# Adaptive-norm transformer block: reduce steps over all units, dense steps in two halves, a fixed table of stages, values and causal rows by DMA

## What is computed

```python
h = _layernorm(x) * (1 + ca) + sa
x = x + ga * attention(h)      # 16 heads of 16, causal, q/k/v/o each w plus a LoRA of rank 16
h = _layernorm(x) * (1 + cb) + sb
x = x + gb * ffn(h)            # relu(base + lora_e) @ Wo.T, the two best of 4 experts, weighted
```

## Time and profile before

| | |
|---|---|
| median of 3 runs | 2076.18 us (2071.84 to 2076.54) |
| profiled execution | 2072.05 us, span 2070.3 us |
| PE, DVE, ACT, POOL busy | 1851.8, 1232.0, 940.3, 507.7 us |
| granted PE clock, mean | 0.96 |

### The profile page before, as it was taken

How to read it: one execution, slowest core, us unless ns; L and a number is a source line. 1 busy time by engine, 2 the same in 40 slices (tenths; PEclk the granted TensorE clock), 3 DMA queues, 4 the chain that set the end, 5 groups by cost and what they waited for, 6 DMA issues and landing times.

```text
span 2070.3 us, 31214 instructions
## 1 busy us (share of the span) xinstructions
PE 1851.8 (89%) x10868; PEld 951.2 (46%) x10868; DVE 1232.0 (60%) x2729; ACT 940.3 (45%) x1701; POOL 507.7 (25%) x803
## 2 busy tenths in 40 slices
PE   5788987999889998899979999799988999799958
PEld 4433443445444454354634545344544545344526
DVE  5666768555774557755585556755578545764241
ACT  1255555444454445544454454544445444454320
POOL 5112211332113321223113221132211332122213
PEclk8879998999999999999999999999999999999979
DMA  4412221121211121111211122012121112110100
GB/s 134 126 42 73 63 57 32 54 68 54 62 45 54 43 86 44 37 62 57 67 32 52 57 65 60 23 56 67 59 58 51 54 65 67 32 32 11 36 0 21
DMA packets 103667, 111.88 MB, mean 54 GB/s; under 512 B 20214, under 2 KB 97618, under 8 KB 103516
## 3 DMA queue, kind: packets, MB, share of 16 engines
q1 hardware_dynamic: 103500, 109.87, 17.8%
q10 hardware_dynamic: 16, 0.02, 0.0%
HBM read 75.72 MB, written 33.58 MB: 53 GB/s over the span
## 4 chain that ended last, share of the span: by engine, by line
PE 65%; DVE 24%; ACT 5%; issue 3%; DMA 1%; SPq 1%; POOL 0%; POOLq 0%; DVEq 0%; ACTq 0%
PE dense L924 10%; PE ov L844 10%; PE st L829 8%; PE mxs L813 7%; DVE negm L1235 6%; PE dense L935 5%; DVE negm_left L1235 5%; PE dense L859 5%; PE dense L901 5%; PE dense L909 4%; PE dense L794 3%; ACT probs L983 3%; PE mxs L817 2%; DVE stats L1087 2%; DVE second L1303 1%
## 5 line engine op out<-in xcount | busy, mean ns | idle before, releaser
L983 ACT ACTIVATE probs<-st 128x512 f32<-128x512 f32 (+1 forms) x1216 | 665.4, 576 | 543.2 <-PE st L829 537.1
L1235 DVE TENSOR_REDUCE negm<-mxs 128x1 f32<-128x384 f32 (+4 forms) x736 | 431.5, 614 | 176.9 <-PE mxs L817 175.1
L829 PE MATMUL st<-q_st,k_st 98*128 98x512 bf16 (+3 forms) x1536 | 455.2, 337 | 29.0 <-ACT probs L983 14.9
L813 PE MATMUL mxs<-k_st,q_st 96*128 96x512 bf16 (+3 forms) x1280 | 400.8, 328 | 57.3 <-DVE negm L1235 33.7
L1235 DVE TENSOR_REDUCE negm_left<-mxs 128x1 f32<-128x512 f32 x512 | 334.7, 683 | 101.6 <-PE mxs L813 98.6
L844 PE MATMUL ov<-probs,v_g 128*32 128x512 f32 (+3 forms) x3072 | 337.9, 511 | 4.7 <-POOL probs L703 4.6
L813 PEld LDWEIGHTS mxs<-k_st,q_st 96*128 96x128 bf16 x1280 | 126.6, 99 | 334.3 <-DVE negm L1235 154.9
L924 PE MATMUL dense<-c_t,wi_t 128*128 128x512 f32 x512 | 245.3, 601 | 0.7 <-ACT ratio_b L1035 0.7
L700 POOL TENSOR_TENSOR fence<-fence 128x1 f32<-128x1 f32 x256 | 49.8, 194 | 736.7 <-ACT probs L983 736.5
L716 POOL TENSOR_TENSOR hid<-hid,second 128x512 f32<-128x512 f32 x128 | 160.9, 1273 | 281.3 <-DVE second L1303 281.3
L829 PEld LDWEIGHTS st<-q_st,k_st 98*128 98x128 bf16 x1536 | 142.3, 100 | 172.3 <-ACT probs L983 72.0
(11 more groups left out here) (167 smaller groups left out, 1728.3 us busy)
## 6 DMA issues: line engine op xcount, KB each, us to landing
q_st<-q_parts_scratch SPq DMA_DIRECT2D x384, 64.0 KB
k_st<-k_parts_scratch SPq DMA_DIRECT2D x384, 64.0 KB
q_parts_scratch<-q_part SPq DMA_DIRECT2D x16, 768.0 KB, 3.3
k_parts_scratch<-k_part SPq DMA_DIRECT2D x16, 768.0 KB, 4.8
xin<-in_L_attn_x SPq DMA_DIRECT2D x9, 1024.0 KB, 5.5
x<-in_L_attn_x SPq DMA_DIRECT2D x8, 1024.0 KB, 5.7
out_x<-ob SPq DMA_DIRECT2D x64, 128.0 KB, 1.7
q_st<-m_row SPq DMA_DIRECT2D x128, 4.0 KB
```

Source lines behind the costliest of these rows:

```text
L813: last = nc.tensor.matmul(mxs[:, bank_m, j * n:j * n + left], q_st[0:KS, slot, h0 + j, qt * P:(qt + 1) * P], k_st[0:KS, slot, h0 + j, k0:k ...
L829: last = nc.tensor.matmul(st[:, score_bank(ch, kt, h0), j * n:(j + 1) * n], k_st[0:KS + 2, slot, h0 + j, kt * P:(kt + 1) * P], q_st[0:KS + ...
L983: nc.scalar.activation(probs[:, par, h0:h0 + heads, 0:n], st[:, score_bank(ch, kt, h0), 0:heads * n].rearrange("p (j q) -> p j q", q=n), A ...
L1235: nc.vector.tensor_reduce(dst[:, h0:h0 + heads], src, axis=AX.X, op=ALU.max, negate=True).then_inc(max_free, 1)
```

## The change

Maxima: `unit_maxima` spreads the 39 steps over all 12 units. Ten steps over half 0 only (`SHORT_STEPS`) now stand in units 9, 10 and 11 of the group before the one in which they stood, and in unit 0; the other 29 in units 1 to 8.

Dense steps are opened and closed apart: `pa`/`pj`, `va`/`vp`, `oa`/`op` are the two halves of a step with other steps between them, `fa`/`fx`/`fb` the three parts of the hidden layer, the last one often in the next unit (`held`). An open step keeps its bank.

Stages stand in units fixed by tables. Norm 1 of a batch is done one body earlier, in units 39 to 46 of the body before. Values are written by ACT to `v_rows`, stored to HBM (`vs`), and loaded as `v_g` by four DMAs of 64-byte pieces per group, at unit 3. The residual addition of `op` goes to POOL. `x1` and the gates are loaded in halves, the first half at unit 34 of the body before. The causal rows go into the stacks by two DMAs that ACT issues. Scaling in the norm stays on DVE, as y*x + b in place of (x - m)*y, with one tiny instruction more for b.

```diff
-VG_UNIT = 8
+VG_UNIT = 2
...
+def unit_maxima(u, first_batch, lead):
+
+    g, k = divmod(u, NU)
+    steps = max_steps()
+    if 0 < k < LATE_MAXIMA or first_batch and g == 0 and k < LATE_MAXIMA:
+        begun = 0 if first_batch and g == 0 else SHORT_STEPS
+        group, part, i, n = g + 1, steps[begun:], k - (begun > 0), LATE_MAXIMA - (begun > 0)
+    else:
+        group, part, i, n = g + 1 + (k > 0), steps[:SHORT_STEPS], (k - LATE_MAXIMA) % NU, NU - LATE_MAXIMA + 1
...
+        for i in range(4):
+            slots[2 + i] += opened("oa", i)
+            chains[4 + i].append(("ls2", i))
+        for i, u in enumerate((7, 8, 8, 8, 9, 9, 9)):
+            chains[u].append(("ln2", i))
+        slots[10] += [("t2", i) for i in range(4)]
+        slots[11] += [("rt",), ("rx",)]
+        for i, u in enumerate((12, 12, 13, 13, 14, 14)):
+            chains[u].append(("ro", i))
...
+        for i, q in enumerate(dense):
+            slots[17 + 30 * i // len(dense)] += q
...
+    if ahead:
+        for i in range(STAT_PARTS):
+            chains[39 + i // 2].append(("ls1", i))
+        for i in range(NORM_PARTS):
+            chains[41 + i // 2].append(("ln1", i))
+        slots[46] += [("t1", i) for i in range(4)]
...
+LATE_MAXIMA = 9
+SHORT_STEPS = 10
+PJ_UNITS = (0, 6, 10, 11, 15)
+PJ_SLOTS = (5, 9, 13)
+V_UNITS = (7, 8, 12, 13)
+PS_UNITS = (17, 36)
...
+                    for j in range(HG):
+                        head = slice((HG * g + j) * DH, (HG * g + j + 1) * DH)
+                        sp.dma_start(v_g[:, g % 2, :, j, 0:DH], rows[:, :, head]).then_inc(vg_in[g % 2], 16)
...
-            for stack, rows in ((q_st, q_rows), (k_st, k_rows)):
-                row_link(nc.gpsimd.tensor_copy(
-                    stack[KS:P, :, :, :].rearrange("p s j (t n) -> p (s j t) n", n=P),
-                    rows.unsqueeze(1).broadcast_to([P - KS, 2 * HG * T, P])))
-            nc.gpsimd.memset(k_st[KS:KS + 2, :, :, :], 1.0).then_inc(ones_ready, 1)
-            pool.wait_ge(ones_ready, 1)
+            row_link(nc.gpsimd.memset(k_rows[0:2], 1.0))
...
+                    if a[0] == 1:
+                        act.wait_ge(rows_chain, ROW_LINKS)
+                        for i, stack in enumerate((q_st, k_st)):
+                            act.dma_start(stack[KS:P, :, :, :].rearrange("p s j (t n) -> p (s j t) n", n=P),
...
-                    nc.vector.tensor_tensor(x1[:, 2 * i:2 * i + 2, :], x1[:, 2 * i:2 * i + 2, :], scaled,
-                                            ALU.add).then_inc(x1_ready, 1)
```

More of the change, by code:

```diff
@@ new lines, in unit_maxima @@
+def unit_maxima(u, first_batch, lead):
[6 more added lines that the diff above has]
+        group, part, i, n = g + 1 + (k > 0), steps[:SHORT_STEPS], (k - LATE_MAXIMA) % NU, NU - LATE_MAXIMA + 1
+    if group >= GROUPS and not lead:
+        return []
+    return [("mx", group % 2, *s) for s in part[len(part) * i // n:len(part) * (i + 1) // n]]
@@ L145, in body_plan @@
-    queue.sort(key=lambda item: item[0])
-    unit_cost = [8 * 512 / 2.4 if kt < 4 * c else 8 * (512 - 128 * (kt % 4)) / 2.4 for c, kt in UNITS]
-    row_maxima = ROW_MAXIMA
+            ffn += [opened("fa", half, ft) for ft in range(8)] + [opened("wa", half, t) for t in range(4)]
+        spare = [opened(*p) for p in pj[len(PJ_UNITS):]] * pre
+        dense = ffn
+        for at, q in zip(PJ_SLOTS, spare):
+            dense = dense[:at] + [q] + dense[at:]
+        for i, q in enumerate(dense):
+            slots[17 + 30 * i // len(dense)] += q
@@ L149, in body_plan @@
+    if ahead and post:
+        extra[3] = ("xin",)
+    if ahead:
+        for i in range(STAT_PARTS):
+            chains[39 + i // 2].append(("ls1", i))
+        for i in range(NORM_PARTS):
+            chains[41 + i // 2].append(("ln1", i))
+        slots[46] += [("t1", i) for i in range(4)]
     plan = []
     if post:
-        plan.append(("xl",))
+        plan.append(("xl", 1))
+    extra[34] = ("xl", 0)
+    held = []
     for u in range(GROUPS * NU):
@@ L239 @@
 ROUTE_PARTS = 6
-def norm_steps(which, first):
-    steps = [("ls" + which, i) for i in range(STAT_PARTS)] + [("ln" + which, i) for i in range(NORM_PARTS)]
-    return [(first + (i + 1) // 3, s) for i, s in enumerate(steps)]
 def chain_steps(names):
@@ L297, in tallied @@
         names.append(f"bank{bank}")
-    if step[0] in DENSE and step[0] not in GOES_ON or step[0] in GOES_ON.values():
+    if step[0] in DENSE and step[0] not in GOES_ON or step[0] in CLOSES:
         names.append("full")
@@ L921, in run @@
                     elif kind == "fa":
[L922 to L928 removed]
+                        hidden(db, 0, *a)
                         return
```

382 lines of the change are left out of this document (202 added, 180 removed).

## The result

The changed kernel takes 1979.29 us (median of 4 runs, 1978.02 to 1980.39), the kernel before 2076.36: ratio 0.9537, 95% interval 0.9521 to 0.9554. I had said 1969, range 1900 to 2040. Direction and size are right; inside the sum one term failed (the last body) and several were off by little.

What follows compares the result with a forecast made beforehand. Two stretches of a middle body were taken as bound by DVE, the rest by PE. 2072.05 - 98 - 2 (seventh body) - 10 + 14 - 8.5 + 0.5 = 1968, plus 1: 1969 us, range 1900 to 2040.

Steps and rivals of the forecast that it cites:

- Middle bodies: Six middle bodies: unit sums fall from 234.3 to 218.0 us, so 16.3 us less each, -98 us in all.
- handovers: Time the unit sums do not see: 9.7 us per middle body, kept whole; 11 us in the last body.
- Last body: Last of the bodies: work sum 195.8 becomes 189.4 us, with 11 us added, -8.5 us (0 and -13).
- First body: First of the bodies: norm 1 of two batches falls into it, +14 us (bounds 5 and 22).
- three stack waits: First body: PE waits for stack loads of units 23, 31 and 35, 3.7, 2.0 and 3.7 us, about 9 together.
- Prologue: Start of the kernel: POOL's causal-row operations go and DVE statistics start earlier, net -10 us (bounds -13 and -5).
- Epilogue: End of the kernel, one chain: POOL adds instead of DVE, only the last add counts, +0.5 us.
- Rival 1: Units 7 to 9 and 12 to 14: DVE stays the bound, 60 us less gain, 2029 us; chance 0.12.
- Rival 2: Middle bodies: evenly spread maxima make the waits between engines vanish, body 214 us, whole 1887; chance 0.10.
- Rival 3: Units 2 to 5: POOL's adds block DVE, +31 us if all 32 hit, 2000 us; chance 0.03.
- Rival 4: Units 3 to 9 of each group: value loads delay stack loads, deciding from 78 ns a piece; slower; chance 0.08.
- Rival 5: Whole kernel: same time as before, from rival 1 and half of rival 4 together; chance 0.04.

Runs made afterwards that it cites:

- stack_window: Changed kernel, but in first and last body maxima needing a stack's second half begin in unit 2, and x1/gate loads follow unit 35's stack load: 1969.3 us.
- last_wide: Changed kernel, but in the last body norm 2 is spread over units 7 to 11, router in 15 to 19, feed-forward from 22: 1973.0 us.
- values_twice: Changed kernel, but each value load is followed by the same load into an unread buffer, and the products wait for both: 1976.3 us.
- norm_early: Changed kernel, but in five bodies VectorE's norm 1 steps stand in units 13 to 18 again, not 39 to 44: 1995.4 us.
- causal_pool: Changed kernel, but the stacks' causal rows are written by two GpSimd copies again, not by two transfers on ACT's queue: 1982.7 us.
- one_moved: Changed kernel with both light-body edits; in middle bodies one projection block moves from unit 11 to 14, the router's last step from 14 to 15: 1953.2 us.
- x1_vector: Changed kernel, but the four x1 additions of each body are done by VectorE again, not by GpSimd: 1976.3 us.
- whole_plan: Changed kernel with both light-body edits; in middle bodies norm 2, router and projections of units 7 to 15 move to where PE has more work: 1972.6 us.

## Why the prediction was right, and where it was not

- **What bounds the kernel.** Right. A body loses its time where VectorE's work exceeds PE's, and the experiments that bring such stretches back bring the time back. The clock is 1.00 in nearly all middle bodies.
- **Middle bodies, -16.3 each.** They gave 14.9. The method (larger of two, plus 9.7 us of handovers) hit the total within 1.5 us: the remainder is 229.1 - 218.0 = 11.1. But its insides were partly luck. Where parts were undone one by one, the sum had priced the norm move well (3.9 against 3.4) and the offload at nothing, rightly, but it gave 1.0 to the maxima, which are worth 5.4, and 0 to the halves, which are worth 3.7. "the split dense steps should shorten them" was in my text, without a price. The sum knows the load of a unit, and neither a chain that must end in it nor a dry ACT.
- **Last body, -8.5.** This is the step that failed: +0.5. I took 189.4 of work plus 11 us of handovers (for which I gave no reason: before, they were 13.2); the remainder was 20.1. Two things were missing. First, the stack load of unit 47 of the body ahead: I had looked at the work between load and reader in middle and first bodies, with 8.8 us at unit 47, but the reader in the last body stands behind a unit 0 without a projection, 2.9 us long instead of 4.2. PE waited 2.0 us at unit 1, and unit 1 took 8.7 instead of 5.1 us; stack_window won 3.8 us there, of which about 2 are left at full clock. Second, I had noted units 7 to 9 and 12 to 14 as VectorE's, but priced them by load alone; without dense work beside them PE waits 2.7 us twice, and what follows mostly ran at a clock of about 0.70. last_wide won 2.4 to 5.8. With both mended the last body takes 200.9 in two kernels and 203.5 in a third, where I had forecast 200.5. Of the 9.0 us that were missing, 3.4 come and go between executions, mostly by the clock (the same plan took 206.1 in values_twice), and 5.2 are what the two edits took off from there to 200.9.
- **First body, +14.** It was +8.9. Of the three stack waits that I had named, those behind the loads of units 31 and 35 came, 6.7 us for the 5.7 that I had for these two. The one behind unit 23 did not, but not because the load was covered: units 23 and 24 ran at a clock of 0.64 and 0.50 and took 9.7 us. In norm_early, where they took 7.0 at 1.00, it came, 2.1 us. By subtraction the evener start gave 8 us (10.5 of work and 6.7 of waits would make 17.2), where I had taken 5: that term was too small, and no run tests it by itself.
- **Prologue, -10.** -9.9, with the reason shown by causal_pool for 8.1 of it.
- **Epilogue.** +1.1 for +0.5, less than its own spread (below), so this term is neither borne out nor refuted.
- **Rivals.** Rival 1 (VectorE remains the bound in its places) holds in the last body and not in the middle ones, whose 229 us are well below 236. Rival 2 did not come, though one_moved goes 2.5 us a body its way. Rival 3: x1_vector found nothing to win back. Rival 4: a piece costs 15.4 ns, a fifth of the 78 from which it would have decided. Rival 5, made of 1 and 4, fell with them.

## What to carry to other kernels

To price a new order, take for each stage the larger of the engines' loads, and then look separately for what this sum cannot see: a chain that has to end in one stage and is read in the next, a block of one engine's work long enough to run another engine dry, and the time between a transfer's issue and its first reader in the shortest stage, not the usual one. Price the light parts of a program (first and last iteration) by themselves, because stages that are short there have nothing to hide a wait behind. When a rearrangement gains nothing, compare it stage by stage: whole_plan hid a gain under two new waits, and one more run, without the longer of them, took 2.5 us a body.
